# GpSimd weight splits, merged digit one-hots and regrouped gathers in a fused adaLN and mixture-of-experts kernel

## The reference, cut to what matters

```python
y = einsum('bfi,oi->bfo', x, W) + fc_bias + z + b          # z: low-rank term of fside
h = gelu(y, approximate=False).reshape(-1, 128)            # 2048 tokens
scores = sigmoid(h @ gate_w.T)
topk_score, topk_ids = top_k(scores.T, 256)                # each expert picks its 256 tokens
xin = h[topk_ids]                                          # gather
eo = silu(xin @ gw.T + gb) * (xin @ up_w.T + up_b)
eo = eo @ down_w.T + down_b
out = zeros_like(h).at[topk_ids].add(eo * topk_score)      # scatter-add
return x + out + shared_expert(h)
```

## Time and profile before

| what | value |
|---|---|
| median of the runs (lowest, highest) | 180.92 us (180.84, 183.15) |
| profiled execution, own time | 182.24 us |
| its span | 180.4 us |
| PE, DVE, ACT, POOL busy | 142.3, 111.9, 93.7, 87.2 us |
| chain that ended last, by engine | POOL 28%, issue 24%, DVE 17%, PE 12%, DMA 10%, ACT 5% |
| scatters (L652) in that chain | 19% |

### The profile page before, as it was taken

How to read it: one execution, slowest core, us unless ns; L and a number is a source line. 1 busy time by engine, 2 the same in 40 slices (tenths; PEclk the granted TensorE clock), 3 DMA queues, 4 the chain that set the end, 5 groups by cost and what they waited for, 6 DMA issues and landing times.

```text
span 180.4 us, 3352 instructions
## 1 busy us (share of the span) xinstructions
PE 142.3 (79%) x1169; PEld 129.3 (72%) x1170; DVE 111.9 (62%) x328; ACT 93.7 (52%) x254; POOL 87.2 (48%) x68
## 2 busy tenths in 40 slices
PE   7698796999879699999999599659950997959400
PEld 2596695998765399989999599659950996949300
DVE  1264899999986489998778457554750376633300
ACT  3369875675421056557687547555650385724200
POOL 0000000000017654767857778787757877781560
PEclk9789999999996999999999879996996599987955
DMA  4899999109804995471342233224223223331320
GB/s 81 293 413 420 409 401 400 48 15 294 245 5 109 323 341 137 90 224 15 49 49 16 47 44 44 37 47 44 37 33 45 32 47 44 33 47 15 29 23 6
DMA packets 16176, 22.71 MB, mean 126 GB/s; under 512 B 1824, under 2 KB 10784, under 8 KB 16032
## 3 DMA queue, kind: packets, MB, share of 16 engines
q1 hardware_dynamic: 10224, 17.90, 28.2%
q0 software_dynamic: 5632, 4.46, 18.5%
q10 hardware_dynamic: 304, 0.14, 0.3%
HBM read 18.17 MB, written 4.33 MB: 125 GB/s over the span
## 4 chain that ended last, share of the span: by engine, by line
POOL 28%; issue 24%; DVE 17%; PE 12%; DMA 10%; ACT 5%; POOLq 1%; SPq 1%; DVEq 0%; ACTq 0%
POOL out L652 19%; POOL rows L642 9%; PE low_banks L469 5%; DMA rows<-h_and_scores,idx 4%; DVE hits L744 4%; DMA out<-y,idx 3%; DVE sh_act L719 3%; DMA xT_sb<-in_xT 2%; PE low_banks L312 2%; DVE cand L767 2%; DVE passed L761 1%; ACT hT L511 1%; PE high_banks L457 1%; POOLq L71 1%; PE high_banks L458 1%
## 5 line engine op out<-in xcount | busy, mean ns | idle before, releaser
L642 POOL DMA_INDIRECT rows<-h_and_scores,idx x32 | 35.5, 1111 | 67.5 <-DVE idx L834 59.0
L652 POOL DMA_INDIRECT out<-y,idx x32 | 51.5, 1608 | 19.9 <-DMA out<-y,idx 8.6
L457 PE MATMUL high_banks<-x_hi,w_hi 128*128 128x256 f32 x128 | 38.8, 303 | 1.0 <-DVE x_lo L850 1.0
L458 PE MATMUL high_banks<-x_lo,w_hi 128*128 128x256 f32 x128 | 37.1, 290 | 0.0
L459 PE MATMUL high_banks<-x_hi,w_lo 128*128 128x256 f32 x128 | 36.9, 288 | 0.0
L457 PEld LDWEIGHTS high_banks<-x_hi,w_hi 128*128 128x128 f32 x128 | 25.7, 201 | 1.3 <-DVE x_lo L850 1.2
L843 DVE SCALAR_TENSOR_TENSOR act<-high_banks,wgu,silu 128x256 f32<-128x256 f32 x44 | 20.1, 481 | 9.5 <-ACT silu L605 7.7
L458 PEld LDWEIGHTS high_banks<-x_lo,w_hi 128*128 128x128 f32 x128 | 25.6, 200 | 0.0
L459 PEld LDWEIGHTS high_banks<-x_hi,w_lo 128*128 128x128 f32 x128 | 25.4, 198 | 0.0
L469 PE MATMUL low_banks<-wd,act 128*128 128x128 f32 x176 | 24.0, 294 | 0.0
L605 ACT ACTIVATE silu<-high_banks,wgu 128x256 f32<-128x256 f32 x44 | 20.0, 469 | 7.4 <-PE high_banks L459 4.8
(11 more groups left out here) (150 smaller groups left out, 253.3 us busy)
## 6 DMA issues: line engine op xcount, KB each, us to landing
wgu<-in_wgu SPq DMA_DIRECT2D x11, 516.0 KB, 12.3
wd<-in_wd SPq DMA_DIRECT2D x11, 256.0 KB, 12.3
h_and_scores<-hrow SPq DMA_DIRECT2D x2, 576.0 KB, 4.3
xT_sb<-in_xT SPq DMA_DIRECT2D x4, 256.0 KB, 4.7
db_sb<-in_down_b SPq DMA_DIRECT2D x1, 1024.0 KB, 8.9
out<-first SPq DMA_DIRECT2D x2, 512.0 KB, 4.9
weff<-in_wgu SPq DMA_DIRECT2D x1, 516.0 KB, 12.7
hrow<-in_wgu SPq DMA_DIRECT2D x1, 516.0 KB, 3.8
```

Source lines behind the costliest of these rows:

```text
L457: pe.matmul(to, w_hi[p][:, w], x_hi[p][:], start=True, stop=False)
L458: pe.matmul(to, w_hi[p][:, w], x_lo[p][:], start=False, stop=False)
L642: pool.indirect_dma_start(rows[e % ROWS_N][:, c, :], None, table, bass.IndirectOffsetOnAxis(ap=idx[:, e, c:c + 1], axis=0)).then_inc(gathe ...
L652: pool.indirect_dma_start(out.rearrange("b p c -> (b p) c"), bass.IndirectOffsetOnAxis(ap=idx[:, e, c:c + 1], axis=0), y_sb[e % Y_N][:, c, ...
```

## The change

- SP issues the first group of `xT_sb` ahead of its two parts of `fs_sb`.
- The contiguous copy `coarse` of the scores' upper halves (ACT) is gone; the counts read the strided halves.
- `upper_weights` of experts 0 and 1 moves on ACT from step 0, step 6 and the end of the bisection into steps 5, 6, 8 and 9.
- `lower_weights` of experts 0 and 1 leaves DVE; POOL does it as eight subtractions of 256 columns in steps 7 to 14.
- POOL gathers once with indices of zero into an unused buffer, as soon as the table stands, ahead of the first real gather.
- `high_is` and `low_is` become one tile `digit_is`, made by one instruction of twice the size; groups of one expert compare with a contiguous `digit1`.
- The group of experts 4 to 7 is split into two groups of two. PE runs `columns(1)` ahead of the last shared output, waits for that output's copy before `grid(2)`, drops the eight products of `keep_warm` there, and runs two instead of six ahead of `transpose_rows(0)`.
- `grid(3)` stands inside `gate_up(0)`. From then on `columns(e + 3)` comes ahead of the transposes, and `grid(e + 4)` stands behind `down(e)`, for e = 0, 1, 2. On DVE `one_hots(e + 4)` and `spread_grid(e + 4)` stand at the end of the turn of expert e.
- Behind each of the first ten experts' scatters come two gathers, then one each; before, every third expert had one.

```diff
-UPPER_STEP, LOWER_STEPS = 6, [1, 7]
+UPPER_STEPS, LOWER_STEPS = [5, 6, 8, 9], [7, 8, 9, 10, 11, 12, 13, 14]
-GROUPS = [(0, 1), (1, 1), (2, 2), (4, 4), (8, 4), (12, 4)]
+GROUPS = [(0, 1), (1, 1), (2, 2), (4, 2), (6, 2), (8, 4), (12, 4)]
...
-            for n in range(2):
-                load_fs(sp, n)
             for g in range(4):
                 sp.dma_start(xT_sb[:, 4 * g:4 * g + 4, :], xT[:, 4 * g:4 * g + 4, :]).then_inc(ld_x[g], 16)
+                if g == 0:
+                    for n in range(2):
+                        load_fs(sp, n)
...
             grid(1)
+            columns(1)
             shared_out(15)
-            columns(1)
-            keep_warm(8)
+            pe.wait_ge(first_ready, B)
             grid(2)
             columns(2)
-            pe.wait_ge(first_ready, B)
-            keep_warm(6)
+            keep_warm(2)
             transpose_rows(0)
             for e in range(E):
-                gate_up(e)
-                if e < 3:
-                    grid(e + 3)
+                gate_up(e, 3 if e == 0 else None)
+                if e < 4:
+                    columns(e + 3)
                 if e + 1 < E:
                     transpose_rows(e + 1)
                 down(e)
                 if e < 3:
-                    columns(e + 3)
+                    grid(e + 4)
...
-            act.activation(coarse[:], halves[:, :, 1], ACT.Copy).then_inc(coarse_ready, 1)
             act.activation(spare[:, 1:2], warm[:, 0:1], ACT.Silu)
-            upper_weights(0, 0)
...
-                if n == UPPER_STEP:
-                    upper_weights(0, 1)
+                if n in UPPER_STEPS:
+                    m = UPPER_STEPS.index(n)
+                    upper_weights(m // 2, m % 2)
...
+            for m, n in enumerate(LOWER_STEPS):
+                w = slice(m % 4 * CAP, (m % 4 + 1) * CAP)
+                pool.wait_ge(w_hi_ready, m // 2 + 1)
+                pool.wait_ge(cand_ready, n + 1)
+                part = pool.tensor_tensor(w_lo[m // 4][:, w], wgu_sb[m // 4][:, w], w_hi[m // 4][:, w], ALU.subtract)
+                if m % 2:
+                    part.then_inc(w_lo_first, 1)
             for n in range(2):
                 pool.wait_ge(table_done[n], 16)
+            pool.indirect_dma_start(rows[ROWS_N - 1][:, 0, :], None, table,
+                                    bass.IndirectOffsetOnAxis(ap=zero_idx[:], axis=0)).then_inc(trial_done, 16)
+            pool.wait_ge(trial_done, 16)
...
-                ahead = 1 if e % 3 == 2 else 2
+                ahead = 2 if e < 10 else 1
...
-                dve.tensor_tensor(by_block(high_is[n % 2], size), high[:, :, None, here].broadcast_to(shape), digits,
-                                  ALU.is_equal)
-                link(dve.tensor_tensor(by_block(low_is, size), low[:, :, None, here].broadcast_to(shape), digits,
-                                       ALU.is_equal))
+                link(dve.tensor_tensor(by_digit(digit_is[n % 2], size), digits_of[:, :, None, here].broadcast_to(shape),
+                                       digits, ALU.is_equal))
...
             for e in range(E):
-                gated(e)
-                if e < 3:
-                    spread_grid(e + 3)
+                if e:
+                    gated(e)
+                if 0 < e < 4:
+                    indices(e + 3)
                 if e + 1 < E:
                     lower_rows(e + 1)
-                if e == 0:
-                    lower_weights(1, 1)
                 if e + 2 < E:
                     lower_weights(e + 2, 0)
                 biased(e)
-                if e < 3:
-                    indices(e + 3)
                 if e + 2 < E:
                     lower_weights(e + 2, 1)
-                if e < 2:
+                if e < 3:
                     one_hots(e + 4)
+                    spread_grid(e + 4)
```

More of the change, by code:

```diff
@@ L116, in moe_program @@
         place_of = sb("place_of", [P, CH], I16)
-        high = sb("high", [P, B, E], I16)
-        low = sb("low", [P, B, E], I16)
+        digits_of = sb("digits_of", [P, 2 * B, E], I16)
         digit = sb("digit", [P, V, E], I16)
+        digit1 = sb("digit1", [P, V, 1], I16)
         number = sb("number", [P, B, E], F16)
@@ L122, in moe_program @@
         tile_at = {n: sb(f"tile_at{n}", [V * n, CT], F16) for n in (1, 2, 4)}
-        high_is = [sb(f"high_is{i}", [P, B * V * 4], F16) for i in range(2)]
-        low_is = sb("low_is", [P, B * V * 4], F16)
+        digit_is = [sb(f"digit_is{i}", [P, 2 * B * V * 4], F16) for i in range(2)]
         numbered = [sb(f"numbered{i}", [P, B * V * 4], F16) for i in range(2)]
@@ L423, in grid @@
                     at = slice(b * V * size, (b + 1) * V * size)
-                    mm = pe.matmul(index_bank(n)[0:V * size, 0:V * size], high_is[n % 2][:, at], numbered[n % 2][:, at],
+                    mm = pe.matmul(index_bank(n)[0:V * size, 0:V * size], digit_is[n % 2][:, at], numbered[n % 2][:, at],
                                    start=(b == 0), stop=(b == B - 1))
@@ L444, in transpose_rows, with gate_up @@
                 tr.then_inc(xin_T, 1)
-            def gate_up(e):
+            def gate_up(e, between=None):
                 p = e % 2
                 pe.wait_ge(x_lo_ready, e + 1)
-                pe.wait_ge(w_lo_ready, e * 2 + 2)
+                if e < 2:
+                    pe.wait_ge(w_lo_first, e * 2 + 2)
+                else:
+                    pe.wait_ge(w_lo_ready, e * 2 - 2)
                 for f in range(FC):
@@ L460, in gate_up @@
                     mm.then_inc(gu_ready, 1)
+                    if between is not None and f == 1:
+                        grid(between)
             def down(e):
@@ L537, in count_third @@
                 with nc.allow_low_precision(reason="integers up to 256"):
-                    data = (coarse[:] if n else halves[:, :, 1]) if n < len(UPPER) else fine[:]
+                    data = halves[:, :, 1] if n < len(UPPER) else fine[:]
                     act.activation(signs[:], data, ACT.Sign,
@@ L580, in _ @@
             shared_behind(STEPS - 1, shared_y, shared_read)
-            for n in range(2):
-                upper_weights(1, n)
             shared_read(13)
@@ L701, in _ @@
             dve.tensor_scalar(digit[:], from_one, -1.0, None, ALU.add)
+            dve.tensor_scalar(digit1[:], from_one[:, :, 0:1], -1.0, None, ALU.add)
             for size in (1, 2, 4):
@@ L732, in _ @@
                 upper = n < len(UPPER)
-                data = (coarse[:] if n else halves[:, :, 1]) if upper else fine[:]
+                data = halves[:, :, 1] if upper else fine[:]
                 first_step = n in (0, len(UPPER))
                 last_step = n in (len(UPPER) - 1, STEPS - 1)
-                if n == 1:
-                    dve.wait_ge(coarse_ready, 1)
                 if n == len(UPPER):
-                    dve.tensor_scalar(higher[:], coarse[:], coarse_at[:], None, ALU.is_gt, ALU.add,
+                    dve.tensor_scalar(higher[:], halves[:, :, 1], coarse_at[:], None, ALU.is_gt, ALU.add,
                                       accum_out=cnt[:, 3:4]).then_inc(higher_ready, 1)
@@ L770, in _ @@
                 elif upper:
-                    dve.scalar_tensor_tensor(fine[:], coarse[:], place[:], halves[:, :, 0], ALU.is_equal,
+                    dve.scalar_tensor_tensor(fine[:], halves[:, :, 1], place[:], halves[:, :, 0], ALU.is_equal,
                                              ALU.mult).then_inc(fine_ready, 1)
@@ L835, in indices, with gated @@
                     "p (e c) -> p e c", c=CT)).then_inc(idx_ready, 1)
-            def gated(e):
-                for f in range(FC):
+            def gated(e, chunks=range(FC)):
+                for f in chunks:
                     dve.wait_ge(silu_ready, e * FC + (f + 1))
```

45 lines of the change are left out of this document (22 added, 23 removed).

## The result

The changed kernel has a median of 188.68 us in four runs (187.44 to 188.88), the kernel before on the same chip 180.88 (180.71 to 183.15). The ratio is 1.039, with a 95% interval of 1.029 to 1.048: slower by 7.8 us. The forecast was 183.7, so the sign and the place are to be looked at apart from the size, which is 5.0 us short. The ratio puts the time at 188.0 (1.039 × 180.92), just inside the stated range of 176.5 to 188.5; the median is 0.2 us above it. "Over 2% slower" had been given 0.38, less than the 0.44 for a change of under 2% either way. Ratios here compare only runs within 1.5% of the fastest of their kernel, so one can differ a little from the quotient of two medians.

A forecast was written before the change was run, and what follows sets the result against it. Bound: the chain up to expert 4's scatters, then POOL alone. An earlier first gate-up (4.1 us) is overspent on PE's waits and clock, +3.65 there; with −0.85 behind, +2.8 on the median of 180.92 gives 183.7 us, range 176.5 to 188.5.

The forecast's parts named there:

- What bounds the kernel: Behind expert 4's scatters POOL alone sets the pace; ahead of that, POOL's first scatter waits for rows, gate-up, indices and `y`.
- The new wait: PE idles about 2.9 to 3.3 us before the grids behind downs 0 to 2; gate-ups follow 10.45 us apart.
- The clock: PE's granted clock falls after each 3 us wait, costing 1.5 us three times and once more in gate-up 0.
- The first gate-up: Gate-up of expert 0 starts at 58.9 us instead of 63.00.
- Rival 1: PE's clock holds through the 3 us waits: 177.7 us, or 177.0 with the start's full 1.6; chance 0.17.
- rival 2: PE's clock does not come back between the waits: +6 us over four turns, 189.7 us; chance 0.10.
- start: With `xT_sb` issued first, PE's wait for it shrinks by nothing to 1.6 us; 0.9 taken.
- bisection, `passed` 0 to 14: Step 1 loses 0.7 us of waiting for ACT, step 6 comes 0.4 later: −0.3 us.
- first one-hots, up to the first idx: Merged compare for the first group saves 0.4 us, partly covered by PE's shared input product: −0.3 us.
- first idx to gate-up: One-hots, grids, spread, columns, two products and transposes between the first idx and gate-up 0: 7.7 us.
- rival 3: POOL's eight weight subtractions hold the bisection's chain: +3.4 us, 187.1 us; chance 0.08.
- The rest: Behind expert 4's scatter: −1.6 for expert 14's wait for `y`, +0.75 for longer landing waits, together −0.85 us.

The follow-up runs named there:

- Experiments 1 and 3: 1: changed kernel with the later grids put back ahead of the transposes, 179.45 us; 3: kernel before with only the change's order of grids, 187.31 us.
- Experiment 2: Changed kernel with 13 keep-warm products on PE in front of each of the three late grids: 184.92 us.
- `gs_fill`: Changed kernel with grids and SP's first issues put back, and keep-warm products set into PE's gaps around the first grids and transposes: 175.37 us.
- `gs_fill5`: The kernel of `gs_fill` timed again: 176.15 us, ratio 0.976 to the kernel before.
- experiment 8: Old order of gathers in the changed kernel with grids, SP's order and keep-warm products put back: 176.76 us, beside the new order there: 176.91 us.
- `b_xt`: Kernel before with only SP's first issues changed, first group of `xT_sb` ahead of `fs_sb`: 181.15 us, ratio 1.009.
- `gs_keep_a0`: Changed kernel with grids, SP's order, keep-warm products and also the old order of gathers put back: 176.76 us, ratio 0.974.
- `gs_keep5`: Changed kernel with grids, SP's order and keep-warm products put back, new order of gathers kept, timed again: 176.91 us, ratio 0.986.

## Why the prediction was right, and where its numbers were not

**What bounds the kernel: held.** With the grids back, POOL's gaps are 0.30 from expert 1's scatters on, up to the landing waits near the end; with the grids late, PE's list sets the pace up to the scatters of expert 3 and POOL's behind them.

**The new wait: the deciding step, and right.** Forecast were waits of 2.9 to 3.3 us and turns of 10.45; measured are 2.58, 3.04 and 3.05, and turns of 10.73 and 10.64 (transposes at 79.38, 90.11, 100.75). The parts listed for e = 0 add up to 5.4 us from gate-up to gate-up, not to the 5.5 that I used, and 5.4 is what the trace has (69.5 to 74.87). Experiments 1 and 3 show it both ways: taken out of the changed kernel the order gives 9 us back, and put alone into the kernel before it costs about 6.

**The clock: right in kind.** A wait of 3 us costs a fall worth 1.5 us; a gate-up of 4.4 to 4.6 us instead of 2.95 is that size. Experiment 2 removes the falls and leaves the waits, and gets 4.2 us of s0 to s4. Rival 1, by which the clock holds, is false by the rows of 0.66, and so is rival 2: the clock was back ahead of each wait, and PEclk from 59 to 95 us was 0.76, where under 0.6 would have decided for it. The one place mis-sized is the first gate-up. Its 6.3 us at 1.2 GHz from end to end, for a forecast of 2.95 + 0.56 + 1.5 = 5.0, is 1.3 more.

**The first gate-up: wrong by 4.3 us.** 58.9 was forecast, and it started at 63.18. By the terms of the sum:

| term | forecast | measured | error |
|---|---|---|---|
| start | −0.9 | +0.95 | +1.85 |
| bisection, `passed` 0 to 14 | −0.3 | +0.8 | +1.1 |
| first one-hots, up to the first idx | −0.3 | −0.2 | +0.1 |
| first idx to gate-up | 7.7 | 8.97 | +1.25 |

*Start.* The wait saved was real, but I held the transfers for independent. My bounds ended at 0, and the chain had two more inputs: `fs_sb` and `cf_sb` were on time only as long as `xT_sb` did not stand ahead of them. From the first `project` to the first `passed` the two traces take the same 10.2 us, so all of the +0.95 stands ahead of it. The lower bound should have been the mirror of the wait that I removed.

*Bisection.* The mechanisms were right. Step 1 is 0.73 shorter (0.7 forecast) and step 6 is 0.28 longer (0.4), and in eight of the nine other traces with the changed bisection the 14 steps take 26.75 us, for 27.15 before: −0.4. In the changed kernel's own profiled execution the granted clock was 0.66 from 31 to 36 us, where the kernel before had 1.00, and a shared product of eight matmuls, 1.14 us there, took 1.82. It delays the sum of the counts behind it:

```profile
31.56 1.82 PE L357 MATMUL low_banks<-hT,sh_sb 128*128 128x128 f32 x8
...
32.31 0.73 POOL L667 TENSOR_TENSOR w_lo<-wgu,w_hi 128x256 fp32r<-128x256 f32 x1 [1.31 <-DVE cand L774]
...
34.33 0.22 DVE L768 TENSOR_SCALAR_CACHE_REDUCE passed<-low_banks,place 128x3 f32<-128x3 f32 x1 [0.72 <-PE low_banks L385]
```

Step 8 takes 2.59 us instead of 1.79, and step 9 is 0.4 longer. The ninth of these traces, `gs_fill`, has 27.97 with the same two long steps, the same product at 1.83 us and again a granted clock of 0.66 (28 to 33 us); `gs_fill5`, the same kernel again, has 26.76. So this is a matter of the execution, and nothing in the trace of before shows when it comes.

*POOL's subtractions, rival 3: false.* Each takes 0.73 us, starts with its step and is over some 0.7 us before the next `cand` of an ordinary step; steps 11 to 14 take 1.84 us as before. By the Trainium skill, "SBUF — State Buffer", section "Who interferes with whom", a DVE instruction with two SBUF inputs contends with a GpSimd instruction that reads SBUF; `cand`, the one such instruction of an ordinary step, does not overlap with the subtraction, and no ordinary step shows a wait: the trace agrees, but does not test the rule. The 0.56 us estimated from the Trainium skill, "GPSIMD Engine Reference", section "Elementwise — side-by-side cycle accounting", was short; the measured 0.73 decides.

*First idx to gate-up.* The merged compares cost 0.69, 1.08 and 1.22 us for 512, 1024 and 2048 elements: the forecast to 0.01. The path up to `grid(2)` is 0.17 longer than taken. From the grid to the end of its `columns` are 2.2 us, for 1.4. It is here:

```profile
58.58 0.55 PE L429 MATMUL low_banks<-numbered,digit_is 128*32 128x32 f16 x16 [0.89 <-ACT first L557]
...
60.10 0.41 DVE L831 TENSOR_TENSOR spread<-low_banks,spread_at 32x256 f16<-32x256 f32 x1 [1.62 <-PE low_banks L429]
...
61.54 0.63 PE L448 MATMUL low_banks<-cf_sb,rows 128*128 128x128 f32 x2
...
63.18 0.58 PE L465 MATMUL high_banks<-x_hi,w_hi 128*128 128x256 f32 x1 [1.00 <-DVE x_lo L856]
```

From the grid's first record to the `spread` that reads it are 1.52 us. In the kernel before they were 0.61, from the grid at 59.09 to:

```profile
59.70 0.41 DVE L825 TENSOR_TENSOR spread<-low_banks,spread_at 32x256 f16<-32x256 f32 x1 [1.10 <-PE low_banks L424]
```

This is the largest part of the 1.25, and its cause stays open (the last section). Transposes to gate-up cost 1.64 for 1.38, at 1.2 GHz. The rows had landed by 58.99, 2.5 us ahead of the transposes: as forecast, the landing doesn't set them, and nothing shows the trial gather to pay. With it the first gather starts 0.78 us behind the end of its idx, without it 0.92.

**The rest: right term, wrong reference.** −0.85 was forecast and −3.3 measured, but the order of gathers isn't shown to be worth more than the term: experiment 8 finds 0.2. Over all traces the rest is 74.5 to 76.3 us in the ten with the new order, and 75.8, 75.9, 77.0 and 78.95 in the four with the old one. Predicted and found are three landing waits near 2 us at the end (1.96, 1.97, 1.94) and no wait for `y` at experts 12 to 15. What was off is the trace that I subtracted from. The kernel before had a landing wait of 1.72 and one for `y` of 3.68; at the same scatters `b_xt`, with the same order, has 0.65 and 2.19. That is 2.6 of the 3.0 us by which its rest is shorter. My sum ran against an execution that was long at its end; the 1.3 us between its own time and the median should have warned me.

**The sum.** Against the profiled execution: 4.3 from the first gate-up, 1.2 from its length and its turn, 0.9 from the next turns and the last `y`, less 2.5 in the rest, make 3.9, which is 187.1 less the forecast span of 183.2. The other 1.1 are the two medians. The sign and the mechanism of the waits were right; the early gain that should have paid for half of them never came. Of its 4.3 us, 1.85 are the start, which the change itself made worse, 1.1 are one execution's clock in the bisection, and 0.8 are the slow return of `grid(2)`, without a known cause. That the total came out at the edge of the range and not beyond it is in part luck: errors of 6.4 us one way met one of 2.5 the other way.

## What to carry to other kernels

An engine that works in order should get work for later only where that work's inputs are ready by then: here a grid whose tokens were gathered 13 us later, and two that were needed later still, held PE for 3 us each, and with it the `y` that POOL waited for. Before taking "idle" products out of a matmul list, price the clock of what comes next; here 12 of them gave the next gate-up 1.5 us and took about 1 us themselves. When a transfer is moved to the front, take the waits of those that it passes as the other bound. And a term read as a difference to one trace needs a second look at whether that trace is usual at that place.

## What the runs showed that I had not expected

- `cf_sb`, issued by ACT's queue at 0.74 us in both kernels, was usable at 2.7 us, or at 4.8 to 5.5 in the four traces where 256 KB stood first on SP's queue: the order on one queue moved another queue's transfer by 2.1 to 2.8 us.
- From a grid's first matmul to its reader are 0.6 to 0.7 us in three traces and 1.2 to 2.05 in the others, for the same grid of experts 2 and 3. The clock doesn't sort them: `gs_fill` has 2.0 at a granted clock of 1.00, and `gs_keep_a0` has 0.61 and `gs_keep5` 1.51 with the same list there. The cause stays open; it is worth up to 1.4 us of the path.
- The scores come at 13.7 to 17.3 us in the seven traces of the changed code with `fs_sb` first, all with the same code up to there. That is more than any edit tried here moved, apart from those at the late grids, and it goes into the time of every run.
